# Who issues the closed tiles' stores, and how the step words are read, in a four-layer graph network kernel

## The reference, cut to what matters

```python
x = layernorm(x + L0(x))    # attention over edges, 8 heads
x = layernorm(x + L1(x))    # two rounds of: h = x @ W; sum over edges of h[src] * norm; layer norm, relu
x = layernorm(x + L2(x))    # relu(segment_sum((x @ W)[src] * edge_weight, dst) + b)
x = layernorm(x + L3(x))    # messages from two projections of x[src], softmax over edges, 4 heads
# the core of every one of them:
msg = table[src] * something_per_edge
out = segment_sum(msg, dst, num_segments=6250)
```

## Time and profile before

| | us |
|---|---|
| median of 3 runs | 5310.72 |
| lowest and highest | 5306.38, 5313.35 |
| the profiled execution: span | 5313.9 |

### The profile page before, as it was taken

The page is one execution under the profiler, slowest core; times in us unless marked ns, Lnnn a source line. Parts: engine busy times, 40 slices in busy tenths (PEclk is TensorE's granted clock), DMA queues, the critical chain, the costliest instruction groups (busy, mean ns, idle before and its releaser), DMA issues.

```text
span 5313.9 us, 86764 instructions
## 1 busy us (share of the span) xinstructions
PE 3931.6 (74%) x13357; PEld 2389.2 (45%) x13357; DVE 3517.2 (66%) x10780; ACT 2554.6 (48%) x6938; POOL 3875.0 (73%) x3995
## 2 busy tenths in 40 slices
PE   6888888887777777677777777777677656666763
PEld 4666666664444444344444443343333333444442
DVE  6789888885554545444444445666666578888887
ACT  1667667664555555455545552000000166666665
POOL 3777777775777777677777776777777677777775
PEclk8889889988899998887777777877888777777776
DMA  5444444443333333443333333333333322222222
GB/s 151 113 122 126 122 126 124 120 121 98 111 112 112 111 112 111 118 139 111 111 112 112 111 112 100 109 109 109 109 108 109 98 57 57 57 57 57 57 57 68
DMA packets 252628, 549.14 MB, mean 103 GB/s; under 512 B 71467, under 2 KB 136235, under 8 KB 252108
## 3 DMA queue, kind: packets, MB, share of 16 engines
q0 software_dynamic: 178752, 478.34, 32.8%
q1 hardware_dynamic: 66972, 58.64, 3.5%
q10 hardware_dynamic: 6384, 6.62, 0.5%
HBM read 501.16 MB, written 42.15 MB: 102 GB/s over the span
## 4 chain that ended last, share of the span: by engine, by line
PE 32%; POOL 22%; DMA 18%; issue 13%; DVE 6%; ACT 6%; SPq 2%; DVEq 1%; ACTq 0%; POOLq 0%
PE bank L1453 18%; POOL scratch L1863 12%; DMA scratch<-tab_x,src_idx 10%; POOL scratch L1399 9%; DMA scratch<-tab_h,src_idx 7%; PE bank L1297 4%; PE bank L172 4%; PE bank L1154 3%; DVE reg_acc L1463 2%; ACT scratch L1066 2%; POOL reg_x L1024 2%; SPq L865 1%; DVE reg_acc L1322 1%; PE bank L1142 1%; PE bank L157 1%
## 5 line engine op out<-in xcount | busy, mean ns | idle before, releaser
L1453 PE MATMUL bank<-scratch 128*128 x4986 | 1946.5, 501 | 739.9 <-SPq L1414 356.6
L1463 DVE TENSOR_TENSOR reg_acc<-reg_acc,bank 128x256 f32 x2493 | 1047.3, 420 | 1368.2 <-PE bank L1453 1310.3
L1399 POOL DMA_INDIRECT scratch<-tab_x,src_idx x1566 | 1494.3, 954 | 533.5 <-issue 259.4
L1453 PEld LDWEIGHTS bank<-scratch 128*128 128x128 f32 x4986 | 961.2, 229 | 1630.2 <-issue 1582.6
L1024 POOL DMA_INDIRECT reg_x<-tab_h,src_idx x832 | 838.7, 1008 | 302.7 <-issue 184.1
L1399 POOL DMA_INDIRECT scratch<-tab_h,src_idx x783 | 746.6, 953 | 264.7 <-issue 153.0
L1863 POOL DMA_INDIRECT scratch<-tab_h,src_idx x783 | 743.0, 949 | 249.3 <-issue 226.8
L1916 PE MATMUL bank<-reg_w,scratch 128*128 128x260 f32 x1664 | 639.8, 527 | 282.7 <-issue 180.1
L1423 ACT ACTIVATE scratch<-iota_row,dst_loc 128x128 f32<-128x128 f32 x1662 | 579.6, 393 | 345.5 <-PE bank L1453 336.1
L1297 PE MATMUL bank<-reg_x,scratch 128*128 128x265 f32 x1664 | 582.4, 461 | 72.7 <-DVE reg_x L1339 70.4
L1916 PEld LDWEIGHTS bank<-reg_w,scratch 128*128 128x128 f32 x1664 | 376.3, 252 | 505.1 <-issue 305.0
(11 more groups left out here) (313 smaller groups left out, 4364.1 us busy)
## 6 DMA issues: line engine op xcount, KB each, us to landing
scratch<-tab_x,src_idx POOLq DMA_INDIRECT x1566, 2.8
scratch<-tab_h,src_idx POOLq DMA_INDIRECT x1566, 2.7
reg_x<-tab_h,src_idx POOLq DMA_INDIRECT x832
tab_h<-scratch ACTq DMA_DIRECT2D x7, 924.0 KB, 5.2
reg_x<-in_x SPq DMA_DIRECT2D x7, 896.0 KB, 11.3
reg_w<-in_x SPq DMA_DIRECT2D x49, 128.0 KB, 2.3
tab_x<-reg_acc SPq DMA_DIRECT2D x49, 128.0 KB
tab_xs<-reg_w SPq DMA_DIRECT2D x49, 128.0 KB, 2.6
```

The costliest lines, as they stand in the source:

```text
L1399: e.indirect_dma_start(ring_rows[:, j % SLOTS, :], None, self.table, bass.IndirectOffsetOnAxis(ap=src_idx[:, j:j + 1], axis=0)).then_inc(* ...
L1453: e.matmul(self.bank(i), ring_hots[:, i % HOTS, :], rows, start=True, stop=True).then_inc(*self.product.up)
L1463: e.tensor_tensor(v, v, self.bank(i), ALU.add).then_inc(*self.added.up)
```

## The change

In layers 1 to 3 SyncE's queue loses the stores; `sync` only waits for landings and counts them, and `STORE_AT` is gone. ScalarE issues each store itself: behind its own copy it waits for the copy's semaphore and then issues the DMA. The step words are read as 16-bit halves: the row is viewed as U16, a load fetches 32 halves for 16 steps, each in a register of its own, and the masking and the shift fall away. SyncE's loads of `ends_row` in layer 4 (14 values) read only the low half of each word, with a stride of two.

```diff
+        slot_halves, end_halves = slot_row.bitcast(U16), ends_row.bitcast(U16)
...
         def load_slots(e, name, t0):
             if name not in slot_regs:
-                slot_regs[name] = ([e.alloc_register(f"slot{k}") for k in range(GROUP)],
-                                   [e.alloc_register(f"part{k}") for k in range(2)])
+                slot_regs[name] = [e.alloc_register(f"slot{k}") for k in range(2 * GROUP)]
             n = min(GROUP, STEPS_PAD - t0)
-            e.load(slot_regs[name][0][0:n], slot_row[:, t0:t0 + n])
+            e.load(slot_regs[name][0:2 * n], slot_halves[:, 2 * t0:2 * (t0 + n)])
         def slot_rows(e, name, t, a, b):
-            words, parts = slot_regs[name]
-            e.reg_alu(parts[0], words[t % GROUP], PLACES - 1, op=ALU.bitwise_and)
-            v = e.snap(parts[0], min_val=0, max_val=(SLOTS - 1) * FEAT)
+            v = e.snap(slot_regs[name][t % GROUP * 2], min_val=0, max_val=(SLOTS - 1) * FEAT)
             return scratch[:, bass.DynSlice(v + a if a else v, b - a)]
         def chunks_needed(e, name, t):
-            words, parts = slot_regs[name]
-            e.reg_alu(parts[1], words[t % GROUP], 16, op=ALU.logical_shift_right)
-            return e.snap(parts[1], min_val=1, max_val=POSITIONS)
+            return e.snap(slot_regs[name][t % GROUP * 2 + 1], min_val=1, max_val=POSITIONS)
...
-            e.load(end_regs[0:n], ends_row[0:1, c0:c0 + n])
+            e.load(end_regs[0:n], end_halves[:, 2 * c0:2 * (c0 + n):2])
...
-            def sync(self, e, table, taken, stored, at):
-                done = 0
-                for j in range(POSITIONS + 1):
-                    while done < T and STORE_AT[done] == j:
-                        e.wait_ge(*taken(done))
-                        e.dma_start(node_rows(table, done, done + 1), at(done)).then_inc(*stored[done % len(stored)].up)
-                        done += 1
-                    if j < POSITIONS:
-                        e.wait_ge(*self.got[j % ARRIVALS](j // ARRIVALS))
-                        e.sem_inc(*self.landed_n.up)
+            def sync(self, e):
+                for j in range(POSITIONS):
+                    e.wait_ge(*self.got[j % ARRIVALS](j // ARRIVALS))
+                    e.sem_inc(*self.landed_n.up)
...
                         e.mul(sums[:, k, :], dense2.out(k), dinv[:, k:k + 1]).then_inc(*taken2.up)
+                        e.wait_ge(*taken2(k))
+                        e.dma_start(node_rows(tab_h2, k, k + 1), acc[:, k:k + 1, 0:FEAT]).then_inc(*h2_stored.up)
...
                         e.copy(staged[:, k % 2, :], dense_l2.out(k)).then_inc(*taken_l2.up)
+                        e.wait_ge(*taken_l2(k))
+                        e.dma_start(node_rows(tab_x2, k, k + 1),
+                                    staged[:, k % 2:k % 2 + 1, :]).then_inc(*x2_stored[k % 2].up)
...
                         e.copy(staged[:, k % 2, 0:ROW3], dense_l3.out(k)).then_inc(*taken_l3.up)
+                        e.wait_ge(*taken_l3(k))
+                        e.dma_start(node_rows(tab_h3, k, k + 1),
+                                    staged[:, k % 2:k % 2 + 1, 0:ROW3]).then_inc(*h3_stored[k % 2].up)
```

More of the change, by code:

```diff
@@ L9 @@
 I32 = mybir.dt.int32
+U16 = mybir.dt.uint16
 ALU = mybir.AluOpType
@@ L65 @@
 PARTS = 16
-STORE_AT = [min(WHOLE[k] + PARTS + 3 - k, POSITIONS) for k in range(T)]
 NI, NF = 4, 3
@@ L1565, in close1_sync @@
         def close1_sync(e):
-            edges1.sync(e, tab_h2, taken2, [h2_stored], lambda k: acc[:, k:k + 1, 0:FEAT])
+            edges1.sync(e)
         bias2, gamma2, beta2, bias_l2 = (reg_w[:, k * FEAT:(k + 1) * FEAT] for k in (0, 1, 2, 5))
@@ L1602, in pass2_sync @@
             load_x(e, tab_xs, x1_back)
-            edges2.sync(e, tab_x2, taken_l2, x2_stored, lambda k: staged[:, k % 2:k % 2 + 1, :])
+            edges2.sync(e)
         def weights3_tensor(e, n):
@@ L1747, in pass3_sync @@
         def pass3_sync(e):
-            edges3.sync(e, tab_h3, taken_l3, h3_stored, lambda k: staged[:, k % 2:k % 2 + 1, 0:ROW3])
+            edges3.sync(e)
         def pass3_tensor(e):
```

## The result

| | before | after |
|---|---|---|
| median of 4 runs, us | 5312.03 | 5862.61 |
| lowest and highest | 5306.38, 5318.47 | 5860.63, 5877.51 |
| span of the profiled execution | 5313.9 | 5860.3 |

The changed kernel takes 1.1045 times as long [1.103, 1.1061], some 551 us more. Ratios stand here with their 95% interval and can differ from the quotient of the two medians by up to 0.001. The forecast was no change.

What follows compares the result with a forecast made beforehand. GpSimd's gathers were taken to bound layers 1 to 3, and layer 4 to keep GpSimd's pace. The terms 0 + 0 - 0.4 + 0.1 + 0 + 0.3 gave 0.0 us: 5310.7 us, no change, range 5304 to 5317.

Steps and rivals of the forecast that it cites:

- GpSimd's gathers bound the kernel before: Layers 1 to 3: one gather per 1.25 us, 783 a pass, sets the pace and hides the other engines' work.
- SyncE loses its waits and issues: 0: Layers 1 to 3: SyncE loses 3.4 us of waits and 47 us of issue, all beside GpSimd's gathers; value 0.
- ScalarE issues the stores: 0: Layers 1 to 3: 49 stores a layer take 20 us on ScalarE, covered by 480 us of idle time; value 0.
- Rivals A: Layers 1 to 3: SyncE's stores made TensorE and then GpSimd late; 333 us come back, 4978 us; chance 1%.
- B: Layers 1 to 3: SyncE's store issues lengthen the gathers by 11.6 us, which the change removes, 5299 us; chance 6%.
- D: Layer 1: ScalarE's store issue blocks, at 12 us a store +108 us, 5419 us; chance 1%.
- The join from 1 to 2: -0.4 us: Between layers 1 and 2: SyncE's parameter loads begin 0.43 us earlier, and this chain sets the 13th gather; -0.4 us.
- full queue: Start of layer 2: issuing SyncE's seven loads of x took 17.62 us because the queue was full.
- The joins from 2 to 3 and 3 to 4: +0.1: Between the later layers: ScalarE's issue takes 0.366 against 0.32 us, a 0.03 us hop falls away; +0.1 us together.
- The step words on TensorE: Layers 1 to 3: load of 32 registers takes 1.67 us, between -0.6 and +1.1 us a group, 2.3 us waited anyway; value 0.
- The step words in layer 4: VectorE has least room: -0.1 to +0.5 us a group, covered by 2.3 us; +0.3 us after the last gathers.
- Rival C: Layer 4: the load of halves is dear and VectorE bounds the pass; at worst 6.6 us a load, +135 us, 5446 us; chance 4%.

Runs made afterwards that it cites:

- the last experiment: Kernel before with stores moved to ScalarE, words kept 32-bit, and five of SyncE's seven layer 2 loads of x issued inside layer 1: 5305.32 us, 0.9992.
- the mixed load: Kernel before, but TensorE loads 16 low halves with stride two besides the 16 words and does no masking: 5462.47 us, 1.0284.

## Why the prediction was wrong, point by point

1. *GpSimd's gathers bound the kernel before.* Right. In the kernel with the stores moved the four stretches stay within 3 us of the earlier trace rows, and 2.2 us of loads a group on TensorE change nothing.

2. *SyncE loses its waits and issues: 0. ScalarE issues the stores: 0.* Right, both together 1.0001 [0.9992, 1.0011]. A store's issue on ScalarE took 0.326 us in the median in layer 1, where 0.366 was taken. Rivals A, B and D are out: this kernel would have been 333 or 11.6 us shorter or 108 us longer. 11.6 us are 0.2%, and the interval, 0.9992 at the lowest, excludes that too.

3. *The join from 1 to 2: -0.4 us.* Too small to be measured, but its parts moved otherwise. With only the stores moved, the first gather came 20.9 us after the last one of layer 1 instead of 19.3, and the 13th waited 6.4 us instead of 7.3 (one profile each). Whether the 1.6 us come from SyncE's loads beside the store is not shown: the kernel with two word loads, whose stores are SyncE's as before, has 21.5 and 7.8 us there. That SyncE's loads of x set the 13th gather is shown by the last experiment: issued early, the wait is gone. That experiment also bears on the "full queue" of the prediction:

```profile
L1569 SPq DMA_DIRECT2D reg_x<-tab_xs x5: 359/360/380, 1365.5 to 1871.8; - x5
```

   Issued singly in mid-pass the same loads take 0.360 us each; one behind the other, in the kernel before, the last four took 3.3 to 4.3 us each, and the DMA engines stood at a share of 1.05 to 1.10 meanwhile (2247 to 2262 us). So the issue is held up while transfers are under way; more than that about a queue is not shown.

4. *The joins from 2 to 3 and 3 to 4: +0.1.* With only the stores moved they were 13.8 and 10.2 us, before 13.7 and 11.0. Nothing there.

5. *The step words on TensorE: one load of 32 registers for 1.67 us, cover 2.3 us a group.* **This is the step that failed**, in the price of the load. The prediction took two rows, 0.562 us for one register and 1.098 for 16, drew a line through them at 0.036 us a register, and carried it from 32-bit words to 16-bit halves as if only the number of registers counted. The line had no such meaning. On TensorE one word costs 0.318 us when measured by itself and four cost 0.338 (why VectorE's one word took 0.562 stays open); the price goes by fetches, as far as the rows show, and the change takes the loads from four words a fetch to one half a fetch. Measured: 7.54 us. The upper bound, "split in two is twice 1.1", is just the experiment of two loads of words, and it costs nothing, as the prediction said of it. The bound was right about words and did not bound halves.

   The cover was mis-sized too, though this alone would not have mattered. Each group's load grew by 7.54 - 1.11 = 6.43 us, 334 us a pass, of which layer 1 and its join show 277, layer 2 and its join 42, layer 3 and its join 7. What was hidden is therefore 57, 292 and 327 us, or 1.1, 5.6 and 6.3 us a group, with what the saved maskings gave back in it. The prediction had 2.3 us a group from TensorE's wait for SyncE's count, and looking at that wait pass by pass would not have helped: it was 104.8, 134.9 and 115.8 us, or 2.0, 2.6 and 2.2 us a group. The wait is not the room. In layers 2 and 3 part of the room stood in the busy time itself. These are the edge products of layers 1 and 2, in the kernel before and in the changed one (busy us, mean ns, idle before):

```profile
L1453 PE MATMUL bank<-scratch 128*128 x1656 | 573.9, 449 | 222.7 <-SPq L1414 104.8 <-DVE reg_acc L1463 66.7 <-issue 32.5
L1453 PE MATMUL bank<-scratch 128*128 x1658 | 693.1, 534 | 240.8 <-SPq L1414 134.9 <-DVE reg_acc L1463 77.1 <-ACT scratch L1428 10.9
...
L1442 PE MATMUL bank<-scratch 128*128 x1546 | 544.4, 466 | 426.4 <-SPq L1403 268.7 <-issue 141.8 <-ACT scratch L1417 7.8
L1442 PE MATMUL bank<-scratch 128*128 x1586 | 511.3, 469 | 369.8 <-SPq L1403 281.1 <-issue 86.7
```

   Pressed by the loads, a product of layer 2 takes 469 ns instead of 534, and one of layer 3 480 instead of 519; in layer 1 they took 449 already and take 466. TensorE's busy time of the changed kernel, join included, and 52 loads of 7.54 us come to 803 + 392 = 1195 us in layer 1, 604 + 392 = 996 in layer 2 and 586 + 392 = 978 in layer 3, where gathers and join took 1008, 1006 and 993 us before. By this estimate only layer 1, which has the most dense products, doesn't fit; it gives 187 of its 277 us. The extra 3.80 us of the mixed load say the same: in layer 1 198 us more of loads and 151 us of loss leave 0.9 us a group; in layer 2 all was hidden.

   The saving was put at 1.2 us a group. The fused pair fell from 112 to 38 ns in the changed kernel's trace, and the mask of 32 ns is gone as well, 1.7 us a group in all. No run leaves out the mask and the shift alone, so whether this gave time back stays open.

6. *The step words in layer 4: between -0.1 and +0.5 us a group, tail +0.3.* The same mis-sized load, 7.11 us on VectorE, 6.69 on ScalarE and 2.85 for SyncE's 14 halves, and +225 us for the layer and its end. The three were not changed one at a time, so the share of each is not shown.

7. *Rival C, with 4%,* named this mechanism, its place in layer 4 and even its order of price: 6.6 us as the worst. It had it in one place only. For VectorE 7.11 us gives by its formula (7.11 - 4.0) x 52 = 162 us, and 225 were measured for all three engines: either VectorE's room was smaller than the 4.0 us assume, by 1.2 us a group, or the two others have a part in it. On TensorE in layers 1 to 3, where 331 of the 556 us were lost, the prediction did not carry it through, although the same load stands in three passes there. Its chance was set low on the strength of "VectorE's own 16 registers in 1.098 us", which is a row about words. And SyncE's row, read as 0.116 us a register in the median and 0.206 at the most, is not one price that scatters: its 1.624 us is the middle between 1.372 and 1.877, with 25 loads at 1.16 to 1.18 us below and 25 at 2.87 to 2.88 above. The price of a single element, 0.2 us, stood in the trace of before in half of SyncE's loads.

   The Trainium skill (Runtime: NRT & Kernel Launch, "Instruction fetch mechanics") gives some 200 ns a register for register loads, even in bulk. The prediction held the trace against it. Of these runs, halves agree with it (0.233 us each on TensorE, 0.200 on SyncE, by (6.457 - 0.267) / 31), and so do words with a stride or off a multiple of four; words side by side don't (0.064 us). By that page the estimate was 6.4 us a load and 5435 us in all; the first is near the 6.7 to 7.5 measured, the second counts layer 4 alone.

8. *What would show it right or wrong.* "The load of halves takes 1.6 to 2.2 us" and "a hand-over above 0.3 us in mid-pass" did their work: both failed at first sight. "TensorE's wait for SyncE's count stays above 300 us" was a bad sign to name, since it is 852.4 us now and for another reason.

What stays open: what the fetch is, and why neighbouring words go four at a time. And a part of the loss in layer 1 can't be told apart: TensorE's granted clock fell from 0.91 to 0.83 of full speed there, in the same stretch in which it stood idle for each load.

## What to carry to other kernels

A duration is the price of one form of an instruction. Before it is scaled to another form (element width, stride, count), ask which of these the price could hang on, and look at the single durations where minimum and maximum lie far apart; if the trace has no row of the new form, let the range hold the price of one fetch for each element. Hidden cost is paid at the end of a pass where a deep ring lets one engine lag: look at the joins, and at how much work lies behind the last gather. And a wait is not room: in these passes it was 2.0 to 2.6 us a group, and 1.1, 5.6 and 6.3 us were hidden. Compare, pass by pass, the engine's work when it is pressed plus the new cost with the pace that the pass must keep.

## What the runs showed of the hardware

**Register loads are priced by the fetch.** TensorE, with SyncE's in brackets, us:

| elements | words side by side | words, stride two | halves |
|---|---|---|---|
| 1 | 0.318 (0.293) | | 0.296 (0.267) |
| 2 | 0.552 (0.487) | | 0.529 (0.462) |
| 4 | 0.338 (0.307) | | 0.986 (0.851) |
| 8 | 0.596 (0.530) | | 1.922 (1.652) |
| 16 | 1.107 (0.972) | 3.812 (3.272) | 3.787 (3.252) |
| 32 | 2.132 (1.862) | | 7.520 (6.457) |

All of these start at the first word of a row. Sixteen halves with a stride of two take 3.789 (3.252).

A packed word is thus cheaper to load than its two halves, by 7.54 against 1.11 us for 16 words, and the masks and shifts that it needs, 1.7 us a group on TensorE, take far less than that. For a load that starts at a multiple of four words, three fetches of four and two of one make 0.307 + 2 x 0.222 + 2 x 0.200 = 1.15 us for SyncE's 14 words, with 0.222 from (1.862 - 0.972) / 4; 1.16 to 1.18 were measured. The same load two words further on takes 2.87 to 2.88. SyncE's seven loads of seven words at the end of the kernel before point the same way: 1.10 and 1.15 us for the two that start at word 0 and 28, 1.66 to 1.69 for the five others. So the start of a load is worth aligning, and its length worth keeping to a multiple of four words.

**The load stops its queue, and the wait lists don't name it.** TensorE's instructions behind it stood for 7.2 us; the profile put 852.4 us of TensorE's idle time, most of it of this kind, down to SyncE's count, 119 times, and VectorE's and ScalarE's holes of up to 6.8 and 6.6 us to "issue". A releaser whose number of waits goes down while its total goes up is worth doubting.

**One chip was slower.** The kernel before took 6631.97 us on one and 5310.56 and 5313.20 on the two others. Single instructions took the same (TensorE's load of words 1.104 to 1.106 us, gathers 0.95), but with only the stores moved GpSimd's hand-overs on the first chip were up to 3.6 us long under "issue", where 0.3 us was the longest on the third, and up to 4.0 under "remote", a releaser that the third chip's list doesn't have. The mean granted clock was 0.735 instead of 0.826 of full speed. Each chip was used in one session, so chip and session can't be told apart, and the cause stays open:

```profile
POOL scratch L1404 <- issue: 536.6, 1624, 3.6
...
POOL scratch L1404 <- remote: 304.8, 180, 4.0
```

The three kernels that ran on the first and the third kept their order, and the ratios their size within 1.1% (1.0939 and 1.1044 for the halves).
